# A hand-written schedule of side jobs in the second attention, moved to start each batch's input chain earlier

## What is computed

```python
def _attention(x, wq, wk, wv, wo):      # x: rmsnorm(xn, g1), 8 x 512 x 256
    q = (x @ wq)                        # 16 heads of 16, 4 key/value heads
    k = (x @ wk); v = (x @ wv)
    q = q * cos + _rotate_half(q) * sin
    k = k * cos + _rotate_half(k) * sin
    scores = jnp.einsum('bhqd,bhkd->bhqk', q, k) / jnp.sqrt(16)
    attn = jax.nn.softmax(jnp.where(causal, scores, -jnp.inf), axis=-1)
    out = jnp.einsum('bhqk,bhkd->bhqd', attn, v)
    return out.transpose(0, 2, 1, 3).reshape(B, S, D) @ wo
```

## Time and profile before

| what | value |
|---|---|
| median of 3 runs | 3470.98 us (3469.5 to 3473.81) |
| the profiled execution's own time | 3471.95 us |
| its span, first to last instruction | 3470.2 us |
| TensorE busy in the span | 3213.3 us (93%) |
| mean granted TensorE clock | 0.962 of full speed |
| all steps of the stage, TensorE | from 2311.28 us on, 61.19 us a batch where undisturbed |

### The profile page before, as it was taken

How to read it: one execution, slowest core, us unless ns; L and a number is a source line. 1 busy time by engine, 2 the same in 40 slices (tenths; PEclk the granted TensorE clock), 3 DMA queues, 4 the chain that set the end, 5 groups by cost and what they waited for, 6 DMA issues and landing times. The chain is left out here.

```text
span 3470.2 us, 74087 instructions
## 1 busy us (share of the span) xinstructions
PE 3213.3 (93%) x22696; PEld 2398.4 (69%) x22696; DVE 2348.2 (68%) x6849; ACT 2064.0 (59%) x4943; POOL 1184.7 (34%) x1818
## 2 busy tenths in 40 slices
PE   4999999999999999989999979979999964999995
PEld 3777777676777677768888865546666653888884
DVE  5888887887888788776666655556666626666664
ACT  4777777777777777765555543236566621555553
POOL 4434344444333434443333320042321202334432
PEclk9999999999999999999999999969999967999998
DMA  3222222222222222243333331111111134445545
GB/s 95 59 54 59 52 51 57 59 58 54 59 59 54 58 59 57 55 136 121 131 127 127 133 121 49 39 40 28 32 28 27 27 123 148 118 125 143 128 120 164
DMA packets 175948, 280.43 MB, mean 81 GB/s; under 512 B 32850, under 2 KB 117586, under 8 KB 175826
## 3 DMA queue, kind: packets, MB, share of 16 engines
q1 hardware_dynamic: 161234, 258.94, 26.1%
q0 software_dynamic: 14592, 19.93, 3.5%
HBM read 159.79 MB, written 41.16 MB: 58 GB/s over the span
## 5 line engine op out<-in xcount | busy, mean ns | idle before, releaser
L767 POOL TENSOR_SCALAR at_p<-at_p,at_recip 128x128 f32<-128x128 f32 (+3 forms) x1028 | 533.6, 532 | 868.0 <-DVE at_recip L900 868.0
L815 ACT ACTIVATE at_p<-at_p,at_nmax 128x128 f32<-128x128 f32 (+3 forms) x1030 | 573.6, 557 | 336.4 <-DVE at_nmax L894 324.7
L894 DVE CUSTOM_DVE_ANT_0 at_p<-at_s_ps,at_bias 128x128 f32<-128x128 f32 (+3 forms) x1030 | 497.3, 483 | 208.5 <-PE at_s_ps L1031 199.7
L1031 PE MATMUL at_s_ps<-at_k_twice,at_q 64*128 64x128 f32 (+3 forms) x3090 | 379.4, 350 | 5.2 <-DVE at_nmax L894 4.2
L1860 DVE CUSTOM_DVE_ANT_0 aa_a_ps<-aa_a_ps,aa_hidden 128x128 f32<-128x128 f32 (+3 forms) x512 | 247.2, 507 | 173.6 <-PE aa_a_ps L2024 170.8
L1031 PEld LDWEIGHTS at_s_ps<-at_k_twice,at_q 64*128 64x128 f32 x3090 | 232.2, 185 | 176.7 <-issue 162.7
L1052 PE MATMUL at_o_ps<-at_pT,at_v 128*64 128x512 f32 (+3 forms) x2064 | 306.8, 439 | 0.0
L1760 ACT ACTIVATE aa_pT<-aa_b_ps 128x512 f32<-128x512 f32 (+1 forms) x384 | 196.6, 529 | 175.9 <-PE aa_b_ps L2042 173.1
L526 DVE SCALAR_TENSOR_TENSOR nw_hl<-nw_h,nw_coef_now,nw_hh 128x512 fp32r<-128x512 f32 x192 | 149.8, 780 | 163.1 <-ACT nw_hh L454 163.1
L449 ACT ACTIVATE nw_h<-nw_h_ps,nw_b 128x512 f32<-128x512 f32 x192 | 132.1, 688 | 211.1 <-PE nw_h_ps L553 210.6
L905 DVE COPY at_pT<-at_t_ps 128x128 f32<-128x128 f32 (+3 forms) x512 | 248.9, 486 | 0.0
(11 more groups left out here) (317 smaller groups left out, 7942.7 us busy)
## 6 DMA issues: line engine op xcount, KB each, us to landing
at_k_twice<-at_k_parts SPq DMA_DIRECT2D x260, 256.0 KB, 3.7
w_raw<-in_w_dram SPq DMA_DIRECT2D x57, 768.0 KB
nw_w_raw<-in_w_all_dram SPq DMA_DIRECT2D x26, 1024.0 KB, 5.0
nw_w_raw<-in_w_all_dram SPq DMA_DIRECT2D x52, 512.0 KB, 6.8
nw_xh<-xh_dram SPq DMA_DIRECT2D x10, 512.0 KB, 4.3
nw_xl<-xl_dram SPq DMA_DIRECT2D x10, 512.0 KB, 4.9
at_w_raw<-in_w_heads_dram SPq DMA_DIRECT2D x18, 256.0 KB, 4.4
nw_x<-in_x_dram SPq DMA_DIRECT2D x9, 512.0 KB, 5.9
```

What stands on the lines that cost most here:

```text
L767: pool.tensor_scalar(p, p, recip[:, u:u + 1], 1.0, ALU.mult, ALU.mult).then_inc(scaled, 1)
L815: act.activation(p_sb[:, u, 0:N], p_sb[:, u, 0:N], ACT.Exp, bias=nmax[:, u:u + 1], scale=-1.0, accum_out=total[:, u:u + 1]).then_inc(exped, 1)
L894: dve.tensor_tensor_reduce(out=p_sb[:, u, 0:N], in0=s_ps[u % 2][:, 0:N], in1=bias[:, u % 2, S - N:S], scale=1.0, scalar=BIG, op0=ALU.add, ...
L1031: ins = pe.matmul(s_ps[h][:, 0:N], qst[par][rows, q, at], k_twice[par][rows, k, 0:N], start=(i == 0), stop=(i == 2))
```

## The change

It splits the jobs of a batch over two batches of steps. `x0`, `x1`, `kk`, `q0` and `q1` of batch n + 2 now run in steps 9 to 15 of batch n (`AFTER_NEXT`); `k0` to `k3`, `v` and `p0` to `p7` of batch n + 1 in steps 2 to 13 (`NEXT`). For batch 1 the x jobs go to the end of the prologue and `kk`, `q0`, `q1` to steps 0 and 1 of batch 0 (`SECOND`). No step has two projections (`kk`, `q0`, `q1`, `v`, `out`). The two `out` jobs move from slot 0 to slot 1 of the same steps. SyncE's `exchange` and VectorE's `low_k` and `make_xr` move along. No instruction is added or removed.

```diff
--- before.py
+++ after.py
@@ -1576,24 +1576,29 @@
         block = ctx.enter_context(nc.Block())
         GROUPS = B * KV1
         FIRST = ["x0", "x1", "kk", "q0", "k0", "p0", "p1", "v", "q1", "k1", "p2", "p3", "M0", "k2", "k3", "p4", "p5", "p6", "p7"]
-        NEXT = {(0, 0): "x0", (0, 1): "x1", (1, 1): "q0", (2, 0): "kk", (2, 1): "q1", (3, 1): "v", (4, 0): "k0",
-                (6, 1): "p0", (7, 1): "p1", (8, 1): "p2", (9, 1): "k1", (10, 0): "p3", (11, 0): "k2", (12, 0): "p4",
-                (12, 1): "k3", (13, 0): "M0", (13, 1): "p5", (14, 0): "p6", (15, 0): "p7"}
+        SECOND = {(0, 0): "kk", (0, 1): "q0", (1, 1): "q1"}
+        NEXT = {(2, 1): "k0", (3, 0): "k1", (3, 1): "v", (4, 0): "k2", (4, 1): "k3", (5, 1): "p0", (6, 0): "p1", (6, 1): "p2",
+                (7, 0): "p3", (10, 1): "p5", (11, 0): "p6", (12, 0): "p7", (12, 1): "p4", (13, 0): "M0"}
+        AFTER_NEXT = {(9, 1): "x0", (10, 0): "x1", (11, 1): "kk", (14, 1): "q0", (15, 1): "q1"}
         SAME = {(1, 0): "M1", (5, 0): "M2", (9, 0): "M3"}
-        BEFORE = {(7, 0): "out0", (8, 0): "out1"}
+        BEFORE = {(7, 1): "out0", (8, 1): "out1"}
 
         def side_job(n, s, slot):
 
             at = (s, slot)
             if at in SAME:
                 return n, SAME[at]
+            if at in SECOND and n == 0:
+                return 1, SECOND[at]
             if at in NEXT and n + 1 < B:
                 return n + 1, NEXT[at]
+            if at in AFTER_NEXT and n + 2 < B:
+                return n + 2, AFTER_NEXT[at]
             if at in BEFORE and n > 0:
                 return n - 1, BEFORE[at]
             return None
 
-        ORDER = [(0, name) for name in FIRST]
+        ORDER = [(0, name) for name in FIRST] + [(1, "x0"), (1, "x1")]
         for n in range(B):
             for s in range(STEPS1):
                 ORDER.extend(job for job in (side_job(n, s, 0), side_job(n, s, 1)) if job)
@@ -1672,18 +1677,17 @@
             exchange(0, 0)
             exchange(0, 1)
             place(0)
+            exchange(1, 0)
             place(1)
-            exchange(1, 0)
             exchange(1, 1)
             for G in range(GROUPS):
                 if G + 2 < GROUPS:
                     place(G + 2)
-                n, g = divmod(G + 1, KV1)
-                if g == 0 and n + 1 < B:
-                    exchange(n + 1, 0)
                 pack(G)
-                if g == 0 and n + 1 < B:
-                    exchange(n + 1, 1)
+                n, g = divmod(G, KV1)
+                if g == 2 and n + 2 < B:
+                    exchange(n + 2, 0)
+                    exchange(n + 2, 1)
                 spread_out(G)
             sp.wait_ge(loaded, 32)
             sp.wait_ge(tables_loaded, 48)
@@ -1808,6 +1812,8 @@
             act.wait_ge(loaded, 32)
             for name in FIRST:
                 take((0, name))
+            take((1, "x0"))
+            take((1, "x1"))
             late = None
             for n in range(B):
                 for s in range(STEPS1):
@@ -1936,10 +1942,13 @@
                         for i in range(2, TT):
                             mask(G + 2, h, i)
                     take(side_job(n, s, 1))
-                    if s == 3 and n + 1 < B:
-                        low_k(n + 1)
-                    if s in (9, 10, 14, 15) and n + 2 < B:
-                        make_xr(n + 2, (9, 10, 14, 15).index(s))
+                    if s == 1 and n == 0:
+                        low_k(1)
+                    if s == 13 and n + 2 < B:
+                        low_k(n + 2)
+                    if s in (6, 7) and n + 2 < B:
+                        make_xr(n + 2, 2 * (s - 6))
+                        make_xr(n + 2, 2 * (s - 6) + 1)
             invert(GROUPS - 2)
             invert(GROUPS - 1)
             norm(GROUPS // 2 - 1)
@@ -2093,6 +2102,8 @@
                     score(1, h, i)
                 for name in (("k2",), ("k3", "p4"), ("p5",), ("p6", "p7"))[h]:
                     side((0, name))
+            side((1, "x0"))
+            side((1, "x1"))
             pe.wait_ge(set_up, 4)
             for n in range(B):
                 for s in range(STEPS1):
```

## The result

The changed kernel takes 3481.94 us (median of 6 runs, 3479.69 to 3483.14) against 3470.99 for the kernel before in the same comparison: a ratio of 1.0031, 95% interval 1.0018 to 1.0044. It is slower by 0.3%. That is 1.9 us above the upper end of the range given for 8 in 10 (3460 to 3480), and 4.9 above the forecast's own range (3463 to 3477). The profiled execution took 3482.3 us, its span is 3480.5 us.

What follows compares the result with a forecast made beforehand. TensorE's list bounds the stage, so only waits can be won. Prologue and batch 0 +7, batches 1 to 5 +2, batch 6 -6, clock -4.4 give -1.4: about 3469.5 us, own range 3463 to 3477, 8 in 10 3460 to 3480.

Steps and rivals of the forecast that it cites:

- The waits for k0 and x0: TensorE's waits at two side jobs, 1.86 and 0.54 us on average, were to go.
- VectorE's chain to mask 0: First step of a group: last mask, part, mask 0, third score; takes standing in it were to delay TensorE.
- the first rival: Takes of kk, out0 and xr cost TensorE nothing: 2.6 us a batch shorter, 3454 us in all; chance 0.17.
- a forecast of +7: Prologue and batch 0 together get 7 us longer, with +3 and +11 as ends.
- Step 12 gets kk's two products, 0.68 + 0.69 = 1.37: +1.1: VectorE's take of kk now stands ahead of mask 0 in step 12, which lengthens that step by 1.1 us.
- GpSimd's moves: GpSimd's work starts earlier in the batches; charged nothing, as covered by 2 to 8 us of lead.
- the length less 0.2 us: Charge for a take ahead of mask 0, 0.2 us filling latencies; bounds were nothing and the full length.
- The removed wait takes the two falls with it: -4.4 us: Clock falls in batches 5 and 6 were to vanish with the k0 wait, saving 4.4 us.
- The second rival: The clock falls in new waits of some 1.2 us at masks in steps 8 and 12: 3482 us; chance 0.2.
- a slow prologue: Upper end of the charge for prologue and batch 0, a low clock throughout both: 4 us more.
- the banks change hands at least one slot in time: The two m_ps banks of the side jobs were to be free in time at every job; priced at nothing.

Runs made afterwards that it cites:

- turn_k_later: The changed kernel with GpSimd's turn_k also waiting until VectorE has made the part in step 12; 3470.54 us, ratio 0.9990.
- before_k0_slot1: The kernel before the change with k0 moved from slot 0 to slot 1 of step 4; 3472.91 us, ratio 0.9997.
- paired_all: The changed kernel with kk and q0 in step 11, p6 in 14, out jobs and v in slot 0, k1 in slot 1, later xr; 3456.79 us.
- kk_slot0: The changed kernel with kk in slot 0 and p6 in slot 1 of step 11, swapped; 3476.07 us, ratio 1.0007.

## Why the prediction was wrong, step by step

**What held.** The waits for k0 and x0 went. What was late next was VectorE's chain to mask 0, and the first rival, that masks hide their takes, fell. The undisturbed steps came out as laid down: step 8 6.08 (6.18 forecast), steps 0, 1, 2 and 13 within 0.02, step 14 4.85 (4.84), step 11 3.74 (3.90), batch 6 55.17 (55.3). (By its own terms step 8 is 6.21 and step 11 3.92; the slips change nothing.) Ahead of the first piece and in batch 0 it is +9.6 against a forecast of +7; 1.0 of that is the collision in its step 12 and 1.6 a fall, and without them it is 7.0. Within it the parts are off: ahead of the first piece it is +2.8 where +1.1 was charged.

**The step that failed first: "Step 12 gets kk's two products, 0.68 + 0.69 = 1.37: +1.1", with GpSimd's moves priced "at nothing".** It measured 6.02 - 3.64 = +2.38. The two products cost their full length, 1.36 (the 5.00 of turn_k_later less 3.64), not the length less 0.2 us: nothing of it fills a latency, and the upper bound was the right end. The other 1.02 is the collision, six times a stage: 6.1 us. I priced GpSimd's moves at nothing, for their lead over the jobs that need them, and asked what each was late for, but not what it would run beside. In the kernel before `turn_k` followed kk's take of step 2 into a stretch without a `part`. Moved to step 11, the same add starts exactly at the first step of a group, where `part` comes right behind the take that releases it.

The prediction weighed the rule on this, for xr and for nothing else. The Trainium skill (SBUF — State Buffer, Who interferes with whom) says that a VectorE instruction with two inputs in SBUF contends with a GpSimd instruction that reads SBUF, and that whoever comes second is blocked until the other is over. Here the trace agrees, by 1.20 us instead of 0.18 beside an add of 1.26: `part`'s second instruction has two inputs in SBUF. To look for two inputs alone would not have been enough: `part`'s first instruction has one, and took 0.48 or 0.49 us beside GpSimd in step 4 of the kernel before, in all seven batches that have the job, and up to 1.09 in paired_all.

**The step that failed second: "The removed wait takes the two falls with it: -4.4 us".** The two falls did go, and four others came, 6.4 us. The second rival had this mechanism, at 0.2, and its time of 3482 is where the kernel came out, but that is luck: it took two waits of some 1.2 us for the cause, and it is one wait of 2.50; it priced a fall at 2.2 us, and it is 1.6; and the 4 us that it added for a slow prologue did not come, where the collision's 6.1 did. The argument that I used against it, that the new waits are shorter than the old one, was false for step 12 by the missing 1.02 us, and true without it: turn_k_later has waits of 1.07 and 1.49 us, and no fall. So both failures go back to one omission: without the meeting in step 12 the four falls are gone too.

**A small one.** Step 3 is 4.35 for 3.85: v's 16 matmuls wait 0.27 us for the bank that ScalarE empties of k0, two jobs before (1.9 us in 7 times), where the prediction had the banks change hands at least one slot in time; the rest is more busy time than was charged for k1. With 0.13 more in step 4 it is 0.6 us a batch.

**The sum.** The forecast of -1.4 us, with the collision (+6.1), the four falls (+6.4), 0.4 for what batches 1 to 5 have beyond these and beyond the forecast, and 1.0 behind batch 6, makes +12.5; the stage measured +12.4. The profiled spans differ by 3480.5 - 3470.2 = 10.3, the medians by 10.95; the 2 us between span and stage lie in stages that the change doesn't touch.

turn_k_later shows what is left of the forecast without the collision: 61.6 to 61.8 us a batch where 61.6 was forecast, and a ratio of 0.9990, no change by the bound of 0.2%. That the batch comes out so close is in part luck. Steps 3, 4, 9 and 12 are together 1.0 us longer than laid down (step 12 by 0.26, as the products cost their full length), and steps 6, 7, 8, 10, 11 and 15 together 0.9 shorter, step 10 alone by 0.32.

**Left open.** No kernel was run with the prologue's wait for batch 1's xr taken away, so its share of the +2.8 us ahead of the first piece is read from the trace alone: 0.99 us of wait for xr, then 1.97 us for the eight transposes. Nor was a version tried in which the remaining wait of step 8 (0.38 us) is covered, or one without the meetings of step 4.

## What to carry to other kernels

On an engine that works in order, a side job's take costs its full length where it stands ahead of the result that the busiest engine needs next, and next to nothing where a long job still lies behind it in that engine's list (0.35 us of 1.37 were left here, as much as a meeting with GpSimd cost): pair a job whose take is long with another long one instead of spreading them evenly. When a producer is moved, look up what it releases on every other engine, and what will run beside that: here a VectorE instruction of 0.18 us with two inputs in SBUF, met by a GpSimd add of 1.26, and the clock falls behind the longer wait made the whole loss. And a longer wait can cost more than its length: a microsecond on top of one and a half cost, in this kernel, about one more in lost clock.

## What the runs showed of the hardware that was not expected

A VectorE instruction on 128 x 16 numbers took 1.20 us when it started 0.10 us into a GpSimd add of 64 x 512 and 0.18 when it did not; the masks that started beside the same add kept their times. Wherever an instruction of `part` was lengthened so, it ended 0.02 to 0.04 us after the GpSimd one: 0.46 to 0.48 us when it started 0.16 to 0.18 into one of 0.62, 0.58 when 0.05 into one of 0.61, 1.07 when 0.24 into one of 1.28. So the loss goes by what is left of the GpSimd instruction, not by the length of the one that waits. The last of these, and 0.48 in the kernel before, are `part`'s first instruction, with a single input in SBUF. A reciprocal of the same size beside a GpSimd add kept its 0.24 or 0.25 in all these traces, so not every instruction with one input is lengthened; what makes the difference was not tested.

Falls of TensorE's clock against the longest wait of a batch, in the kernels profiled: 2.50 us gave 4 of 6, 4 of 6 and 5 of 6 batches; 2.29 gave 3 of 6; the kernel before had two falls at its six waits of 1.81 for k0, one of them from 1.2 us into the wait, and none at the one of 2.12, in batch 0; before_k0_slot1 had its one fall behind the one wait of 2.01, in batch 0, and none behind six of 1.71; 1.49 gave none of 6 in three kernels; kk_slot0, with waits of 1.20 and 0.37 in one step, had one of 6. A fall cost about 1.6 us, and the two that lasted 6.83 us some 2.9 each. So the length of the wait is not all that decides, and these are counts of one execution each. How the chance depends on where in a batch the wait stands is not settled by these.
